# A graph layer on one core: gathering plain 512-byte rows and splitting each pair of chunks, in place of a table of split rows

## What is computed

```python
seg = dst * R + edge_type                                  # R = 65
sums = segment_sum(x[src], seg).reshape(N, R, F)           # N = 6250, F = 128
cnt = segment_sum(ones, seg).reshape(N, R, 1)
conv = einsum('nri,rio->no', sums / maximum(cnt, 1), W_rel) + x @ W_root + bias
h = conv + x @ W_res + b_res
h = (h - h.mean(0)) * rsqrt(var(h) + EPS) * gamma + beta   # over the nodes
out = layernorm(x + relu(h))                               # over the features
```

## Time and profile before

| | |
|---|---|
| median of 3 runs | 2403.25 us (2401.85 to 2405.14) |
| profiled execution, span | 2403.0 us |
| TensorE busy | 2051.2 us (85%) |
| VectorE, ScalarE, POOL busy | 1396.7 (58%), 886.1 (37%), 1485.5 us (62%) |
| mean granted TensorE clock | 0.935 |
| moved by transfers | 233.86 MB, mean 97 GB/s |

### The profile page before, as it was taken

One profiled execution on the slowest core, in us unless ns is written; L12 is line 12 of the kernel. 1 busy time (PEld: TensorE's weight loads), 2 busy tenths in 40 slices (PEclk: granted clock), 3 DMA queues, 4 the chain that ended last, 5 costly groups with the idle time before them and its releaser, 6 DMA issues.

```text
span 2403.0 us, 38063 instructions
## 1 busy us (share of the span) xinstructions
PE 2051.2 (85%) x13396; PEld 1898.7 (79%) x13396; DVE 1396.7 (58%) x2444; ACT 886.1 (37%) x1651; POOL 1485.5 (62%) x1582
## 2 busy tenths in 40 slices
PE   5798888888888889889888889888988988888987
PEld 3687878878778878877888778777887877778887
DVE  7575565565556556547557457556556555645645
ACT  4333334333333333333333333333333333333333
POOL 6666666666666666666666666666666666666640
PEclk9999989899999989999989989999999989998999
DMA  8643434444443444444343444443343444343433
GB/s 273 162 90 89 96 88 91 94 90 91 94 93 88 90 96 89 90 96 90 88 97 86 91 95 91 91 96 87 89 96 89 90 92 90 88 91 88 91 69 108
DMA packets 244737, 233.86 MB, mean 97 GB/s; under 512 B 27097, under 2 KB 239491, under 8 KB 243907
## 3 DMA queue, kind: packets, MB, share of 16 engines
q0 software_dynamic: 223056, 203.79, 38.1%
q1 hardware_dynamic: 21491, 27.60, 3.7%
HBM read 218.48 MB, written 12.80 MB: 96 GB/s over the span
## 4 chain that ended last, share of the span: by engine, by line
PE 79%; issue 10%; DVE 4%; another core or an unknown queue 3%; ACT 2%; POOL 1%; DMA 1%; ACTq 0%; DVEq 0%; SPq 0%; POOLq 0%
PE tb L667 39%; PE ps L632 29%; PE ps L636 6%; PE tb L560 4%; DVE onehot L1018 2%; ACT agg L770 2%; POOL wsb L515 1%; DVE same L957 1%; DMA wsb<-in_x_dram,srcT 0%; DVE lst L1206 0%; DMA eth<-in_edge_type_dram 0%; PE tb L610 0%; DVE agg L1230 0%; PE tb L580 0%
## 5 line engine op out<-in xcount | busy, mean ns | idle before, releaser
L525 POOL DMA_INDIRECT xg<-xtab,srcT x1545 | 1458.5, 944 | 824.5 <-issue 359.5
L1018 DVE TENSOR_SCALAR onehot<-iota,segT,vT 128x456 fp32r<-128x456 f32 x1563 | 1086.7, 741 | 673.2 <-PE ps L636 423.4
L770 ACT ACTIVATE agg<-ps 128x390 f32 (+1 forms) x1563 | 842.0, 539 | 1454.7 <-PE ps L636 924.2
L667 PE MATMUL tb<-agg,wsb 128*128 128x138 f32 x6370 | 1212.4, 314 | 181.9 <-issue 140.7
L632 PE MATMUL ps<-onehot,xg 128*128 128x390 f32 (+1 forms) x3126 | 1195.2, 447 | 67.1 <-issue 55.9
L667 PEld LDWEIGHTS tb<-agg,wsb 128*128 128x128 f32 x6370 | 921.6, 202 | 219.8 <-issue 170.4
L632 PEld LDWEIGHTS ps<-onehot,xg 128*128 128x128 f32 x3126 | 626.6, 202 | 117.0 <-issue 103.6
L636 PEld LDWEIGHTS ps<-onehot,xg 128*128 128x128 f32 x3028 | 613.8, 203 | 56.8 <-issue 52.8
L636 PE MATMUL ps<-onehot,xg 128*128 128x66 f32 x3028 | 610.5, 202 | 35.9 <-issue 34.2
L957 DVE SCALAR_TENSOR_TENSOR same<-ps,rel 128x1088 bf16<-128x1088 f32 (+3 forms) x96 | 145.5, 1515 | 0.0
L560 PE MATMUL tb<-same,identb 128*128 128x512 bf16 x416 | 114.4, 400 | 26.5 <-DVE same L957 24.9
(11 more groups left out here) (133 smaller groups left out, 338.2 us busy)
## 6 DMA issues: line engine op xcount, KB each, us to landing
xg<-xtab,srcT POOLq DMA_INDIRECT x1545
xtab<-agg SPq DMA_DIRECT2D x4, 1536.0 KB
hinit<-H SPq DMA_DIRECT2D x1, 3125.0 KB
agg<-in_x_dram SPq DMA_DIRECT2D x4, 768.0 KB, 7.5
out_dram<-agg SPq DMA_DIRECT2D x6, 448.0 KB, 3.0
dsth<-in_dst_dram SPq DMA_DIRECT2D x23, 64.0 KB
eth<-in_edge_type_dram SPq DMA_DIRECT2D x23, 64.0 KB
srcr<-in_src_dram SPq DMA_DIRECT2D x12, 64.0 KB
```

What stands on the lines that cost most here:

```text
L525: pool.indirect_dma_start(out=xg[c % RING][:], out_offset=None, in_=xtab.bitcast(F32R), in_offset=bass.IndirectOffsetOnAxis(ap=srcT[t % 2] ...
L667: ins = nc.tensor.matmul(o, wsb[:, r * F:(r + 1) * F], pair_rhs(p, r), start=(r == 0), stop=(r == R - 1))
L770: nc.scalar.activation(agg_group(g)[:, :, bass.ds(off, n)], ps[c % NRB][:, 0:n * R].rearrange("f (n r) -> f r n", r=R), ACT.Copy).then_inc ...
L1018: nc.vector.tensor_scalar(onehot[o][:].rearrange("p (a b) -> p a b", a=3), iota3[:, :, 0:IW], segT[t % 2][:, k:k + 1], vT[t % 2][:, k:k + ...
```

## The change

All chunks are gathered as plain 512-byte rows of x, and the table is gone. Chunks go in pairs, 782 of them. Pair j lands in one tile of 256 columns: the first nine in the free part of `wsb`, the others in a ring of eight buffers `land`. ScalarE makes the high parts of a pair with one copy of 256 columns, VectorE the low parts with one operation of two inputs, into a ring of five buffers `parts`. TensorE waits for the low part at each even chunk and for no gather. ScalarE makes the high part of pair j behind the evacuation of chunk 2j-5; VectorE makes the low part behind the one-hot of chunk 2j+3; the landing buffer of pair j is free again for pair j+8 when its low part is made. The source numbers of the first tile are loaded first, ahead of all else, and turned before the other numbers are used. ScalarE clears the region where the table's pieces lay. The comparisons stand three chunks apart in place of two, VectorE's from 71; `count` and `weights` at 95 and 97. The late weights have a semaphore of their own, which TensorE waits for at relation 47.

```diff
-RING = 18
+FX = 18
+LAND = 8
+SPLIT = 5
+HI_AHEAD = 3
+LO_BEHIND = 3
+LO_FIRST = 2
-HI_AHEAD = 12
-LO_AHEAD = 4
 PE_CMP = 70
+CMP_STEP = 3
-DVE_CMP = 76
-DVE_SUM = 94
-DVE_W = 96
+DVE_CMP = 71
+DVE_SUM = 95
+DVE_W = 97
...
-        xg = [sb(f"xg{s}", [P, 2 * F], F32R) for s in range(RING)]
+        land = [sb(f"land{s}", [P, 2 * F], F32) for s in range(LAND)]
+        parts = [sb(f"parts{s}", [P, 4 * F], F32R) for s in range(SPLIT)]
...
+        def landed(j):
+            n = pair_chunks(j) * F
+            if j < FP:
+                return wsb[:, (WLO + 2 * j) * F:(WLO + 2 * j) * F + n]
+            return land[(j - FP) % LAND][:, 0:n]
...
+        def part_of_pair(j, part):
+            return parts[j % SPLIT][:, part * 2 * F:part * 2 * F + pair_chunks(j) * F]
...
                 if t == 0:
+                    sp.dma_start(srcr[:], rows(src, a, a + n)).then_inc(src_in, 16)
+                    sp.wait_ge(cleared, 3)
...
-            for q in range(5):
-                sp.wait_ge(lo_rdy, q + 1)
-                sp.wait_ge(hi_rdy, q + 1)
-                if q < 4:
-                    lo, hi = q * XPIECE, (q + 1) * XPIECE
-                    sp.dma_start(xtab[0:XT * P, :].rearrange("(p t) f -> p t f", t=XT)[:, lo:hi, :],
-                                 pieces[:, lo:hi, :]).then_inc(tab_out if q < 3 else tab_rest, 16)
-                else:
-                    sp.dma_start(xtab[XT * P:N, :], pieces[0:NREM, XT, :]).then_inc(tab_rest, 16)
...
-            sp.wait_ge(first_lo, RING)
+            sp.wait_ge(lo_rdy, FP)
...
-                pool.wait_ge(agg_ps, c - RING + 2)
+                if c % 2 == 0 and j >= FP + LAND:
+                    pool.wait_ge(lo_rdy, j - LAND + 1)
                 pool.indirect_dma_start(
-                    out=xg[c % RING][:], out_offset=None, in_=xtab.bitcast(F32R),
-                    in_offset=bass.IndirectOffsetOnAxis(ap=srcT[t % 2][:, k:k + 1], axis=0)).then_inc(gath[c % RING], 16)
+                    out=landed(j)[:, c % 2 * F:(c % 2 + 1) * F], out_offset=None, in_=x,
+                    in_offset=bass.IndirectOffsetOnAxis(ap=srcT[t % 2][:, k:k + 1], axis=0)).then_inc(landed_sem(j)[0], 16)
...
-                if c < RING:
-                    pe.wait_ge(first_lo, c + 1)
-                else:
-                    pe.wait_ge(gath[c % RING], 16 * (c // RING + 1))
+                if c % 2 == 0:
+                    pe.wait_ge(lo_rdy, c // 2 + 1)
...
+                    if p == 0 and r == WLO:
+                        pe.wait_ge(w_late, 16)
...
+            def high_parts(j):
+                act.wait_ge(*landed_sem(j))
+                nc.scalar.activation(part_of_pair(j, 0), landed(j), ACT.Copy).then_inc(hi_rdy, 1)
...
+            for lo, hi in ((XS0, XZ), (XZ, XN0)):
+                nc.scalar.activation(agg[:, lo:hi], ones[:, 0:1].to_broadcast([P, hi - lo]), ACT.Copy,
+                                     scale=0.0).then_inc(agg_clear, 1)
+            for j in range(HI_AHEAD):
+                high_parts(j)
...
-            act.wait_ge(tab_out, 16 * 3)
+            act.wait_ge(agg_clear, 2)
...
                 evacuate(c, offs[c % 4])
-                if c + HI_AHEAD < RING:
-                    first_rows(c + HI_AHEAD)
+                if c % 2 == 1 and c // 2 + HI_AHEAD < NP2:
+                    high_parts(c // 2 + HI_AHEAD)
...
+            def low_parts(j):
+                dve.wait_ge(hi_rdy, j + 1)
+                nc.vector.scalar_tensor_tensor(out=part_of_pair(j, 1), in0=landed(j), scalar=1.0,
+                                               in1=part_of_pair(j, 0), op0=ALU.mult, op1=ALU.subtract).then_inc(lo_rdy, 1)
...
+            dve.wait_ge(src_in, 16)
+            nc.vector.tensor_copy(srcf[:], srcr[:]).then_inc(srcf_rdy, 1)
+            dve.wait_ge(src_ps, 1)
+            nc.vector.tensor_copy(srcT[0][:], turn[:, 2 * P:3 * P]).then_inc(src_rdy, 1)
...
-            split(4)
+            for j in range(LO_FIRST):
+                low_parts(j)
             count(0)
...
                 one_hot(c)
-                if c + LO_AHEAD < RING:
-                    first_rest(c + LO_AHEAD)
+                if c % 2 == 1 and c // 2 >= LO_FIRST + LO_BEHIND // 2:
+                    low_parts(c // 2 - LO_BEHIND // 2)
```

More of the change, by code:

```diff
@@ L177, in gnn @@
         XN0 = XS0 + XST
+        XZ = XS0 + XST // 2
         XN1 = XN0 + (XT + 1) * F
[L179 to L181 removed]
+        assert XN0 >= PREG and XN1 + 512 == AGG >= 2 * PREG
         xnat = agg[:, XN0:XN1].rearrange("p (t f) -> p t f", f=F)
@@ L184, in gnn @@
         head = agg[:, 0:XS0]
-        WLO = R - RING
-        first_x = wsb[:, WLO * F:R * F].rearrange("p (c f) -> p c f", f=F)
+        WLO = R - FX
+        NP2 = ceil_div(NCH, 2)
+        FP = FX // 2
+        assert FX % 2 == 0 and SPLIT >= HI_AHEAD + 2 and LO_FIRST <= HI_AHEAD
         xTs = [xT, rest[:, 0:512], head[:, 0:512]]
@@ L249, in gnn @@
         src_rdy = sem("src_rdy")
-        first_hi = sem("first_hi")
-        first_lo = sem("first_lo")
+        first_in = [sem(f"first_in{j}") for j in range(FP)]
         rows_rdy = sem("rows_rdy")
@@ L263, in gnn @@
         oh_rdy = sem("oh_rdy")
-        gath = [sem(f"gath{s}") for s in range(RING)]
+        land_in = [sem(f"land_in{s}") for s in range(LAND)]
         agg_ps = sem("agg_ps")
@@ L630, in own_sum @@
                 def own_sum(part):
-                    rows = rows_in_sbuf(c)[:, part * F:(part + 1) * F]
-                    return nc.tensor.matmul(bank[:, 0:w], rows, onehot[o][:, 0:w], start=(part == 0), stop=(part == 1 and not carried))
+                    return nc.tensor.matmul(bank[:, 0:w], rows_in_sbuf(c, part), onehot[o][:, 0:w], start=(part == 0), stop=(part == 1 and not carried))
                 def carry_sum(part):
-                    rows = rows_in_sbuf(c - 1)[:, part * F:(part + 1) * F]
-                    return nc.tensor.matmul(bank[:, 0:R + 1], rows, onehot[(c - 1) % NOH][:, W6:W6 + R + 1],
+                    return nc.tensor.matmul(bank[:, 0:R + 1], rows_in_sbuf(c - 1, part), onehot[(c - 1) % NOH][:, W6:W6 + R + 1],
                                             start=False, stop=(part == 1))
@@ L654, in transform @@
                     if p == 0:
[L655 removed]
+                        pe.wait_ge(w_in, 16)
                     if p == 1:
@@ L817, in _ @@
             root_up(5)
-            for c in range(4, HI_AHEAD):
-                first_rows(c)
-            act.wait_ge(tab_out, 16 * 3)
+            act.wait_ge(agg_clear, 2)
             offs = ()
@@ L1057, in _ @@
                 compare(0, 2 * q + 1)
-                split(q)
                 if q == 1:
@@ L1067, in _ @@
             columns_of(0)
-            for c in range(LO_AHEAD):
-                first_rest(c)
             offsets_of(0)
@@ L1101, in _ @@
                     nc.vector.tensor_scalar(col(BAD), tcol[:, 10:11], 0.0, None, ALU.is_gt).then_inc(bad_rdy, 1)
+            for j in range(NP2 - 1 - (LO_BEHIND // 2 - (1 - NCH % 2)), NP2):
+                low_parts(j)
             dve.wait_ge(bad_ps, 1)
```

86 lines of the change are left out of this document (30 added, 56 removed).

## The result

| | before | after |
|---|---|---|
| median of the runs | 2404.19 us | 2624.34 us (2616.43 to 2639.04) |
| ratio | | 1.092 (95% interval 1.089 to 1.096) |
| span of the profiled execution | 2403.0 us | 2623.7 us |
| granted clock of TensorE, 200 to 2300 us | 0.93 | 0.88 |

The changed kernel is 9.2% slower. The forecast was 2387, in a range that ended at 2445.

The account below looks back on a forecast made before the run. The prediction took TensorE to bound the steady part, slowed by something unexplained beside gathers. Terms of -8.5, +8, -6 and -10 gave -16.5 from 2403.0, so 2387 us; its own range was 2355 to 2398, with rivals 2270 to 2445.

Parts of the forecast that it names:

- The step that failed: Gathers in the steady part: buffers freed by low parts eight pairs back, lead some 20 us, so nothing late.
- Start, -8.5: Kernel start: without the table and with source numbers first, evacuation 0 comes 9.5 us earlier, 8.5 us kept.
- Group heads, +8: Transform at each group's head: a high part in ScalarE's backlog delays 33 groups by 0.25 us each, +8 us.
- Comparisons, -6: Comparisons three chunks apart are ready when TensorE comes; of its 19.5 us wait less than a third kept, -6 us.
- Less traffic, -10: Steady part: gathers of 512 bytes a row relieve TensorE slightly, -10 us, within bounds of 0 and 505 us.
- High and low parts: Per pair 0.40 us on ScalarE, 418 ns on VectorE; bounds 0 to 78 us for the chain, taken as 0.
- The port: Low parts on VectorE lengthen GpSimd's gathers by at most 0.34 us per pair, to 1.42 us per chunk; costs nothing.
- Traffic was the brake: Steady part: halved gather bytes give back much of 505 us; 2221 us, or 2310 with half the way. Chance 0.25.
- The chain of parts decides: TensorE's wait at even chunks: the low part is last, 78 us slower, 2465, or 2425 with half. Chance 0.28.
- The floor that it named: GpSimd's gathers at 1.25 to 1.42 us per chunk limit any relief; 2221 us worked out with 1.33.
- its sign of recognition: TensorE waiting in front of chunks for the low part, more than 30 us in total.
- Nothing but noise: Whole kernel: start's gain lost again, group heads up to 20 us; 2408 or 2402, within 5 us of 2403. Chance 0.12.

Follow-up runs that it names:

- e9: Changed kernel with each gather from the 19th on also waiting for TensorE's count of chunk c-17: 2478.04 us, ratio 1.018 to the kernel before.
- e3: Kernel before with gathers 18 to 1562 fetching 512 bytes a row, low columns keeping old rows: 2403.66 us, ratio 1.001.
- e6: Kernel before with unread copies on ScalarE and two-input subtractions on VectorE added, each of 256 columns per two chunks: 2406.63 us, ratio 1.001.
- e7: Kernel before with only VectorE's unread two-input subtraction of 256 columns added per two chunks: 2406.60 us, ratio 1.001.
- e14: Kernel before with 6 banks for chunk sums in place of 5, VectorE's keys moved to SBUF: 2087.99 us, ratio 1.026.
- e17: The changed kernel run again, on the chip without held counts: 2060.54 us, ratio 1.014 to the kernel before.
- e1: Changed kernel with the high parts made one pair earlier: 2618.56 us, ratio 1.090 to the kernel before.
- e2: Changed kernel with high parts one pair earlier and low parts behind the one-hot of chunk 2j+1: 2618.60 us, ratio 1.091 to the kernel before.
- e4: Kernel before without gathers from the 19th on, chunks summed from rows already in the buffers: 1846.58 us, ratio 0.769.
- e8: Kernel before without the gathers of odd chunks from the 19th on, half of the gathers: 1846.24 us, ratio 0.768.
- e5: Changed kernel without gathers after the first 34, pairs split again from the landing buffers: 1909.73 us, ratio 0.795 to the kernel before.

## Why the prediction was wrong

**The step that failed** is the one on gathers: "the landing buffer is freed by the low part of eight pairs back ... Nothing is late there." It asked when a gather's rows are needed, and there it was right where counts are held: the second gather of a pair starts 20.8 us ahead of the high part, and no engine waits for rows between 200 and 2500 us. It did not ask what a gather waits for. The unexplained slowing of TensorE, which the prediction had found and left as a fixed 1.477 us, has GpSimd in it. Counts are held while gathers follow one another; GpSimd runs out of permissions to go on and stands still; the bunch of counts lets it go again (next gather 0.2 to 0.3 us behind 216 of 219 bunches). The change put ScalarE's evacuation, the high part and the low part, each in its engine's order, between the count and that permission, and the next gather starts 1.6 us or more behind most bunches. That was costed at 0 and measured some 180 us (7.5 points, by e9). The pace of the steady part moved by 0.135 us a chunk, where the prediction called itself wrong from 0.03.

**The whole, term by term.**
- *Start, -8.5.* Gathers at 4.89 as forecast, but one-hot 0 at 38.73, where 33 was expected (39.20 before), and evacuation 0 at 40.27, where about 35 was expected (44.47 before). Of VectorE's 7.2 us from the splits next to nothing came through to the one-hot: its waits between the edge data and the first one-hot grew from 0.9 to 6.8 us, 2.53 us of them the bias sum's for its load. The 4.2 us at evacuation 0 lie within the bounds of 3 to 12 and come from the wait for the table that is gone.
- *Group heads, +8.* TensorE's wait for the evacuation ahead of a transform rose from 32.7 to 50.3 us, in 18 waits. Right in sign; beside the rest it can't be told apart.
- *Comparisons, -6.* The wait of 19.5 us is gone from TensorE's list; whatever it gave can't be seen beside the loss, and no run took it alone.
- *Less traffic, -10.* Zero: e3, 1.001.
- *High and low parts.* 403 and 418 ns, as costed from the earlier trace rows. Both together cost 4 us as dead work beside held counts (e6).
- *The port.* A gather grew from 944 to 958 ns, far from the bound of 0.34 us per pair. It "costs nothing today, and it is the floor if TensorE gets faster": both halves held. Beside held counts 27 ns more a gather cost 4 us (e7, 971 ns); where GpSimd is the floor they cost their whole length (e14, e17). The Trainium skill ("SBUF — State Buffer", section "SBUF: two separate sides") says that a VectorE operation with two SBUF inputs and a GpSimd operation that reads SBUF exclude each other from a shared port pair for a whole instruction. The trace of e14 agrees in direction: gathers beside such comparisons took 1.22 us against 0.94. In size it is less than a whole comparison of 1.5 us for each, 48.6 us for 96 comparisons, about 0.5 us each; and in e17 a gather that a low part of 0.42 us overlapped took 0.97 us against 0.95.

**The rivals.** *Traffic was the brake* is refuted by e3, and the faster time that it promised never came. The floor that it named, GpSimd at 1.25 us a chunk, is real on the other chip, though the 2221 us worked out for it, with 1.33 us a chunk and 49 us of group heads, was too high: the kernel before takes 2033 us there. *The chain of parts decides* had the sign, and its sign of recognition came true (94.0 us, over 30), but e1 and e2 refute its mechanism: with the low part early ahead of TensorE nothing is won. Its dearest price, 78 us, was a third of the loss. The same chain of parts was late, ahead of GpSimd. *Nothing but noise* is out with the interval of 1.089 to 1.096.

**What stays open.** Why TensorE's counts are held at all, and why on three chips and not on the fourth. That it takes gathers close behind one another is shown (e4, e8). Whether GpSimd's pause lets the counts out or only follows from their absence isn't. Every one of the 59 bunches of the changed kernel came at least 0.8 us behind the end of the last gather, which fits the first, but a wider spacing with all gathers kept wasn't run, and the runs with 4 and 6 banks fell on the chip without held counts. Nor is it split how much of the 180 us lies in the longer way from count to gather and how much in the later pause that e9's expectation names: e9 changes both. Of e5's 63 us no part was taken alone; TensorE waits there for low parts again (23.1 us between 200 and 1700). No version that does all of the work beat the kernel before by more than 0.1%.

## What to carry to other kernels

When the thing that frees a buffer is changed, follow the wait that it releases: what stands ahead of the new signal in each engine's order, and how soon after a stall of the loop it can come. An engine at 57% busy can set the pace, if it pauses each time for a chain of three engines. Here it paid to let the prefetch wait for the consumer at the end of the chain as well (e9), though that is one wait more. It did not pay to make the parts that free the buffer one pair or one chunk earlier (e1, e2). Both were seen only where counts are held. And a slowing found in the trace without a cause is not a constant: give it a rival of its own in which the change feeds it.

## What the runs showed of the hardware

- The same kernel took 2402 to 2437 us on the three chips of three series and 2033 to 2036 on that of two more, with the same instructions. On the first, while gathers are issued every 1.25 us, TensorE's counts stay away ahead of a bunch for 2.9 us in the median and 6.2 at the most (kernel before); on the other there is no such bunch. Without gathers, or with half of them, the first take 1846, and between 200 and 1700 us TensorE is granted 1.00 (the higher of its two levels, 2.4 GHz). The ratio of the change was 1.092 on the one and 1.014 on the other.
- Where counts are held, TensorE is idle more and its clock is lower too. The lower level (1.2 GHz) was granted for 313 us of the kernel before, for 653 us of the changed kernel, and for 60 us of the changed kernel on the chip without held counts (e17). Busy time of TensorE in the changed kernel was 2166.7 us at a mean granted 0.88 and 1911.7 us at 0.99 in e17; one transform matmul took 327 against 301 ns in the mean.
- An indirect gather of 128 rows costs GpSimd 0.94 us and 0.30 us to the next, with 512 bytes a row as with 1024. It is the least time per chunk of this kernel, 1.25 us against TensorE's 1.12.
- A VectorE operation with both inputs in SBUF lengthens a gather beside it: 1.22 us against 0.94 where a comparison of 1.5 us overlapped it (e14), 0.97 against 0.95 with a low part of 0.42 us (e17).
- In the traces, most holds last near a multiple of 0.71 to 0.72 us (2.16, 2.89, 3.59, 4.27, 5.68). No run explains that.
